# Attention's matmuls in pairs, a division on VectorE, unit lists from padded tables

## The reference, cut to what matters

```
h = relu(layernorm(x));  h = (h @ W.T).reshape(n, 8, 32)
enc   = relu(edge_attr @ edge_W.T + edge_b)            # 3 attributes per edge
alpha = sum(h[src]*a_src) + sum(h[dst]*(a_dst + enc))  # per edge and head
alpha = leaky_relu(alpha, 0.2)
ex    = exp(alpha - segment_max(alpha, dst)[dst])
out   = segment_sum(h[src] * ex / max(segment_sum(ex)[dst], 1e-10))
x = x + out + bias
h = relu(layernorm(x))
x = x + relu(concat(h, y1, y2) @ Wfc + bfc)            # y1, y2: two convolutions with batch norm
```

## Time and profile before

| | |
|---|---|
| median of 3 runs | 6951.39 us (6950.96 to 6955.41) |
| profiled execution, its span | 6959.5 us |
| PE, POOL, DVE, ACT busy | 69%, 71%, 51%, 30% of the span |
| unit lists | 0 to 119.5 |
| first dense stage | 119.5 to 308 |
| attention | 308 to 2614 |
| second dense stage | 2614 to 2808 |
| convolutions and end | 2808 to 6959.5 |

### The profile page before, as it was taken

The page is one execution under the profiler, slowest core; times in us unless marked ns, Lnnn a source line. Parts: engine busy times, 40 slices in busy tenths (PEclk is TensorE's granted clock), DMA queues, the critical chain, the costliest instruction groups (busy, mean ns, idle before and its releaser), DMA issues. The chain is left out here.

```text
span 6959.5 us, 113181 instructions
## 1 busy us (share of the span) xinstructions
PE 4805.8 (69%) x27409; PEld 3529.7 (51%) x27410; DVE 3523.0 (51%) x8745; ACT 2073.8 (30%) x5831; POOL 4908.5 (71%) x4806
## 2 busy tenths in 40 slices
PE   2699999999999994555555555556666666666655
PEld 1466666666666664344444444445544544444443
DVE  6688888888888888222222222223222222222224
ACT  3567777777777774000000000001000000000001
POOL 1777777776776756677777777774677777777775
PEclk9899999999999997555555555555555555555555
DMA  6777776777776655211111111111211111111115
GB/s 207 250 210 211 210 215 207 211 212 212 212 213 210 209 175 158 82 52 52 51 52 52 51 52 51 52 51 43 53 33 34 34 33 34 34 34 33 33 26 161
DMA packets 515795, 783.25 MB, mean 113 GB/s; under 512 B 143367, under 2 KB 392452, under 8 KB 514956
## 3 DMA queue, kind: packets, MB, share of 16 engines
q0 software_dynamic: 176176, 377.82, 21.0%
q1 hardware_dynamic: 303390, 369.82, 16.6%
q10 hardware_dynamic: 35758, 30.37, 1.4%
HBM read 695.07 MB, written 82.51 MB: 112 GB/s over the span
## 5 line engine op out<-in xcount | busy, mean ns | idle before, releaser
L1690 POOL DMA_INDIRECT c_g<-conv_table,c_idx x3128 | 3010.6, 962 | 1128.3 <-issue 952.9
L1767 PE MATMUL c_sums<-c_g,acc 128*128 x7040 | 1976.1, 441 | 1714.2 <-SPq L1653 1077.4
L1767 PEld LDWEIGHTS c_sums<-c_g,acc 128*128 128x128 f32 x7040 | 1626.4, 322 | 2220.1 <-issue 2210.1
L1002 POOL DMA_INDIRECT acc<-gat_table,ga_idx x1564 | 1615.8, 1033 | 653.0 <-issue 458.2
L1731 DVE TENSOR_TENSOR acc<-acc,c_sums 128x128 f32 (+1 forms) x1760 | 448.5, 255 | 2838.1 <-PE c_sums L1767 2821.7
L1386 PE MATMUL ga_sums<-ga_wg,ga_S 128*128 128x265 f32 x3520 | 999.3, 406 | 7.1 <-DVE ga_wg L1260 6.0
L1336 PE MATMUL ga_dstp<-ga_oht,ga_h 128*128 128x256 bf16 x5280 | 729.9, 275 | 76.0 <-DVE ga_prod L1181 69.7
L1386 PEld LDWEIGHTS ga_sums<-ga_wg,ga_S 128*128 128x128 f32 x3520 | 610.4, 193 | 171.4 <-issue 65.3
L1336 PEld LDWEIGHTS ga_dstp<-ga_oht,ga_h 128*128 128x128 bf16 x5280 | 505.7, 98 | 344.4 <-DVE ga_prod L1181 130.1
L1181 DVE SCALAR_TENSOR_TENSOR ga_prod<-acc,ga_a_dst,ga_dstp 128x512 f32<-128x512 f32 x880 | 645.0, 733 | 8.0 <-issue 6.7
L1077 ACT ACTIVATE ga_S<-iota_row,ga_dcol 128x128 f32<-128x128 f32 x1760 | 605.0, 392 | 73.5 <-issue 70.6
(11 more groups left out here) (253 smaller groups left out, 3731.5 us busy)
## 6 DMA issues: line engine op xcount, KB each, us to landing
ga_h<-h_parts SPq DMA_DIRECT2D x880, 192.0 KB
ga_dl<-dl_rows SPq DMA_DIRECT2D x110, 512.0 KB
c_g<-conv_table,c_idx POOLq DMA_INDIRECT x3128, 2.5
acc<-gat_table,ga_idx POOLq DMA_INDIRECT x1564
h_parts<-h_split SPq DMA_DIRECT2D x14, 1344.0 KB, 5.2
gat_table<-h_out SPq DMA_DIRECT2D x14, 952.0 KB
x_rows<-md_x SPq DMA_DIRECT2D x14, 896.0 KB, 7.1
fc_x<-x_rows ACTq DMA_DIRECT2D x98, 128.0 KB
```

The source lines that it names most:

```text
L1002: pool.indirect_dma_start(G[:, (v * PC + j) * HROW:(v * PC + j + 1) * HROW], None, gat_table, bass.IndirectOffsetOnAxis(idx[:, c:c + 1], 0 ...
L1690: pool.indirect_dma_start(G[:, c % (2 * SLOTS), :], None, table, bass.IndirectOffsetOnAxis(idx[:, c:c + 1], 0)).then_inc(rows_in[c // 2 % ...
L1767: last = nc.tensor.matmul(sums[:, b % R, 0:width], S[:, u * CH + 2 * b + j, :], flat[:, bass.ds(slots[b] * (2 * width) + j * width, width) ...
```

## The change

**Unit lists.** dst, `prev` and the attributes are no longer loaded and stored by way of SBUF. ACT issues copies from DRAM to DRAM into two padded tables, `pair_rows` (dst and prev of a pair, 2048 bytes) and `attr_pairs` (3072 bytes). SP loads only the last node of each pair (`tail_i`, 777 elements of 4 bytes) and src. POOL gathers seven times 128 rows of the one table, then of the other. The attributes are split behind the gathers, in whole tensors instead of halves.

**Dense routine.** rstd and shift have their own columns for each group, so `normal` no longer waits for earlier relus and copies nothing.

**Attention.** Only PE's `slot` is rewritten: steps of two. All other engines keep their order. Slot by slot PE has the same instructions.

**Second dense stage.** `share`, the multiplication by 1/denominator, goes from POOL to DVE, one group ahead. ACT copies `hT` for tiles 0 to 5 and DVE for tile 6.

**Counts.** `low_halves` reads the lower 16 bits of 32-bit numbers in three register loads.

```diff
+def low_halves(tab):
+    halves = tab.bitcast(U16)
+    return AP(halves.tensor, halves.offset, [list(halves.ap[0]), [2, tab.shape[-1]]])
...
-                for t, a, w in tables:
-                    sp.dma_start(t[0:PADDED, :], a[0:PADDED * UEPP * w].rearrange("(p e) -> p e", e=UEPP * w)).then_inc(s_loads, 16)
...
-                sp.wait_ge(s_rows, 3)
-                sp.dma_start(edge_rows.rearrange("(p q) e -> p q e", q=UQ), rows[:, :, :]).then_inc(s_rows_out, 16)
+                    sp.dma_start(tail_i[0:UFULL, :].rearrange("p (q o) -> p q o", o=1), AP(d.tensor, PAIR - 1, [[UEPP, UFULL], [PAIR, UQ], [1, 1]])).then_inc(s_tail_in, 16)
...
+                act.dma_start(pair_rows[0:FULL, 0, :], d[0:FULL * PAIR].rearrange("(p e) -> p e", e=PAIR)).then_inc(s_pairs, 16)
+                act.dma_start(pair_rows[1:FULL, 1, :], d[PAIR - 1:FULL * PAIR - 1].rearrange("(p e) -> p e", e=PAIR)).then_inc(s_pairs, 16)
...
+                act.dma_start(attr_pairs[0:FULL, :], a3[0:FULL * PAIR * 3].rearrange("(p e) -> p e", e=PAIR * 3)).then_inc(s_attr, 16)
...
-                pool.wait_ge(s_rows_out, 16)
                 pool.wait_ge(s_pair, 1)
+                pool.wait_ge(s_pairs, 16 * 9)
                 for q in range(UQ):
-                    pool.indirect_dma_start(rows[:, q, :], None, edge_rows,
+                    pool.indirect_dma_start(rows[:, q, :, :].rearrange("p n e -> p (n e)"), None, pair_rows.rearrange("u n e -> u (n e)"),
                                             bass.IndirectOffsetOnAxis(pair_i[:, q:q + 1], 0)).then_inc(s_gathered, 16)
+                pool.wait_ge(s_attr, 16 * 4)
+                for q in range(UQ):
+                    pool.indirect_dma_start(given[:, q, :], None, attr_pairs,
...
+                part(0)
+                store(0)
+                for n in range(TURNS, 2 * TURNS):
+                    take(n)
+                part(1)
+                store(1)
+                part(2)
+                store(2)
...
             def normal(g):
-                u = g % 2
                 dve.wait_ge(s_sd, g + 1)
-                if g >= 2:
-                    dve.wait_ge(relu_done, GT * (g - 1))
...
                 def slot(x, a, b, c, tail, more):

                     t, m, v = x.at(), x.at(-1), x.odd(-1)
-                    for k in range(QS):
-                        if k == 0 and tail:
-                            add(x.at(-3), UL - 1)
-                        if k and c:
-                            add(x.at(-2), k - 1)
+                    for k in range(0, QS, 2):
+                        for n in (k - 2, k - 1):
+                            if k == 0 and tail:
+                                add(x.at(-3), UL + n)
+                            if k and c:
+                                add(x.at(-2), n)
                         if b and k == 2:
                             lines(m)
                         if b and k == 4:
                             carries(m, v)
-                        if a and k < QS - 2:
-                            quantum(t, k + 2)
-                        if more and k >= QS - 2:
-                            quantum(t + 1, k + 2 - QS)
-                        if a and k % 2:
-                            dot(t, k - 1)
-                            dot(t, k)
                         if b and k == 6:
                             factors(m)
                             turn_back(m)
+                        for q in (k + 2, k + 3):
+                            if a and q < QS:
+                                quantum(t, q)
+                            if more and q >= QS:
+                                quantum(t + 1, q - QS)
+                        if a:
+                            dot(t, k)
+                            dot(t, k + 1)
                     if a:
                         close(x)
...
-                nc.gpsimd.tensor_tensor(heads, heads, spread(den, [[WROW, GT], [HCOLS, HEADS], [0, HDIM]]), ALU.mult).then_inc(scaled, 1)
                 pool.wait_ge(scaled, g + 1)
                 nc.gpsimd.tensor_tensor(heads, heads, spread(bias[:, :], [[0, GT], [HDIM, HEADS], [1, HDIM]]), ALU.add).then_inc(attended, 1)

+        def share(dve, g):
+            heads, den = columns(g)[:, :, :, 1:HCOLS], columns(g)[:, :, :, 0:1]
+            nc.vector.tensor_tensor(heads, heads, spread(den, [[WROW, GT], [HCOLS, HEADS], [0, HDIM]]), ALU.mult).then_inc(scaled, 1)
+
         def pre(dve, g, xg):
+            if g + 1 < GROUPS:
+                share(dve, g + 1)
             dve.wait_ge(attended, g + 1)
...
-by_act=(1, 3, 5)
+by_act=(0, 1, 2, 3, 4, 5)
```

More of the change, by code:

```diff
@@ L152, in gnn @@
         const = (iota_row, part_id, ident)
[L154 removed]
+        units_phase(nc, sb, ps, sem, held, A, const, pair_rows, attr_pairs, enc_parts, lists)
         end_phase()
@@ L271, in _ @@
-                sp.dma_start(prev_i[PADDED:UFULL, :], d[PADDED * UEPP - 1:UFULL * UEPP - 1].rearrange("(p e) -> p e", e=UEPP)).then_inc(s_loads, 16)
-                sp.dma_start(prev_i[UFULL:UFULL + 1, 0:UREST], d[UFULL * UEPP - 1:EDGES - 1].rearrange("(p e) -> p e", p=1)).then_inc(s_loads, 16)
+                d, s = A["dst"], A["src"]
+                sp.wait_ge(s_tail, 1)
+                with nc.allow_non_contiguous_dma(reason="the last node of each pair"):
+                    sp.dma_start(tail_i[0:UFULL, :].rearrange("p (q o) -> p q o", o=1), AP(d.tensor, PAIR - 1, [[UEPP, UFULL], [PAIR, UQ], [1, 1]])).then_inc(s_tail_in, 16)
+                    sp.dma_start(tail_i[UFULL:UFULL + 1, 0:UREST // PAIR].rearrange("p (q o) -> p q o", o=1),
+                                 AP(d.tensor, UFULL * UEPP + PAIR - 1, [[UEPP, 1], [PAIR, UREST // PAIR], [1, 1]])).then_inc(s_tail_in, 16)
@@ L333, in _ @@
                 nc.vector.tensor_copy(part_id[:, :], part_i[:, :])
[L334 to L337 removed]
+                link(nc.vector.tensor_copy(order[:, :], order_i[:, :]))
+                dve.wait_ge(s_tail_in, 32)
+                link(nc.vector.tensor_scalar(last_i[:, :], tail_i[:, :], 7, None, ALU.arith_shift_right))
                 link(nc.vector.tensor_scalar(last[:, :], last_i[:, :], float(TILES - 1), None, ALU.min))
                 nc.vector.tensor_tensor(last[:, :], last[:, :], order[:, :], ALU.add).then_inc(s_end, 1)
[L340 to L346 removed]
                 dve.wait_ge(s_end_in, 16)
@@ L413, in _ @@
             def _(act):
-                act.wait_ge(s_loads, 16 * LOADS)
-                for half in HALVES:
-                    nc.scalar.copy(left[:, half, :, :], attr[:, :].rearrange("p (q e f) -> p q f e", e=PAIR, f=3)[:, half, :, :]).then_inc(s_split, 1)
-                for n in range(PARTS):
-                    for k, half in enumerate(HALVES):
-                        if n:
-                            act.wait_ge(s_left, 2 * (n - 1) + k + 1)
-                        else:
-                            act.wait_ge(s_split, k + 1)
-                        nc.scalar.copy(part(n)[:, half, :, :], left[:, half, :, :]).then_inc(s_part if n < PARTS - 1 else s_rows, 1)
@@ L431, in _, with part, store @@
                     nc.scalar.copy(t[:, :].rearrange("e (p k) -> e k p", k=TURNS)[:, k, :], turn[:, n % 4, 0:P]).then_inc(s_taken, 1)
+                def part(n):
+                    if n:
+                        act.wait_ge(s_left, n)
+                        nc.scalar.copy(parts[:, n, :, :, :], left[:, :, :, :]).then_inc(s_part, 1)
+                    else:
+                        act.wait_ge(s_given, 16 * UQ)
+                        nc.scalar.copy(parts[:, 0, :, :, :], given[:, :, :].rearrange("p q (e f) -> p q f e", f=3)).then_inc(s_part, 1)
+                def store(n):
+                    act.wait_ge(s_part, n + 1)
+                    for f in range(3):
+                        act.dma_start(attr_rows[n * 3 + f, :].rearrange("(p q e) -> p q e", q=UQ, e=PAIR), parts[:, n, :, f, :]).then_inc(s_attr_out, 16)
+                for n in range(TURNS):
+                    take(n)
                 act.wait_ge(s_ew_rest, 1)
@@ L456, in dense_phase @@
     sd = sb(ctx, f"{name}_sd", [P, GT])
-    rstd = [sb(ctx, f"{name}_rstd{u}", [P, GT]) for u in range(2)]
-    shift = [sb(ctx, f"{name}_shift{u}", [P, GT]) for u in range(2)]
+    if keep is None:
+        keep = [sb(ctx, f"{name}_{n}", [P, TILES]) for n in ("rstd", "shift")]
+    rstd, shift = ([t[:, g * GT:(g + 1) * GT] for g in range(GROUPS)] for t in keep)
     if tp is None:
@@ L575, in relu @@
                     act.wait_ge(turn_done, GT * (g - NH) + a + 1)
-                nc.scalar.activation(hn[g % NH][:, a, :], xg[g % NX][:, a, :], ACT.Relu, bias=shift[g % 2][:, a:a + 1],
-                                     scale=rstd[g % 2][:, a:a + 1]).then_inc(relu_done, 1)
+                nc.scalar.activation(hn[g % NH][:, a, :], xg[g % NX][:, a, :], ACT.Relu, bias=shift[g][:, a:a + 1],
+                                     scale=rstd[g][:, a:a + 1]).then_inc(relu_done, 1)
             def copy(n):
@@ L1602, in load_frees @@
```

(2 more changed lines are left out.)

125 lines of the change are left out of this document (61 added, 64 removed).

## The result

The changed kernel takes 7064.14 us (median of 4 runs, 7061.88 to 7076.25) against 6951.18: a ratio of 1.0171, 95% interval 1.0156 to 1.0185. It is slower by 113 us. I had forecast slower, by 27, and 7064 lies above the range of 6875 to 7045. The profiled execution's span is 7074.5, 115.0 above that of before.

A forecast was written before the change was run, and what follows sets the result against it. In attention PE and DVE were taken to wait for each other, so order mattered. 88 − 36 − 25 = +27 us on the profiled 6959.5 gave 6986.5, less the span's 8.1 above the median: 6978, range 6875 to 7045.

The forecast's parts named there:

- 16-bit counts leave as many register loads as before: 0: Counts read into registers, part of the rest: no time gained or lost, 0 us, bounds −5 and +5.
- the loop: Attention: four alternating legs of PE and DVE, through adds, products, flushes and leaky, summing to 21.1 us a slot.
- Attention, +88: Attention: PE's paired order makes flushes wait for adds, +0.8 us in each of 110 slots; bounds −33 and +143.
- Second dense stage, −36: Second dense stage: multiplication moved to DVE, earlier first store, groups of 9.2 us; −36 us, bounds −45 and +5.
- Unit lists, −25: Unit lists: gathers start at 35, phase ends at 94 instead of 119.5; −25 us, bounds −32 and +5.
- 1 (the order costs nothing): Attention: PE is the bound and later flushes vanish in DVE's idle time; 6890 us, 6857 with full saving; chance 24%.
- 2 (POOL first): Second dense stage: POOL takes the shared ports first, about 3.1 us more a group; 7019 us in all; chance 8%.
- 3 (slow small loads): Unit lists: gathers start at 55 instead of 35, so the units gain only 5; 6998 us; chance 7%.
- 4 (7033): Attention: gathers wait longer for free blocks, 1.3 us lost a slot; 7033 us in all; chance 7%.
- my three terms: Attention +88, second dense stage −36 and unit lists −25, summing to +27 us.

The follow-up runs named there:

- single_32max: The changed kernel with PE's attention order of before and ACT's counts loaded as 32-bit numbers with a register maximum, against the kernel before: 6897.6 us, 0.9915.

## Why the prediction was wrong, point by point

- **"16-bit counts leave as many register loads as before: 0".** This is the step that failed, and it carries the miss. The term was 0, with bounds of −5 and +5; alone the load cost 49 us, and with the pairs 75 (7064 − 6989). The prediction counted loads and not their price, and gave as its reason that "no row shows an instruction waiting for them". There was one: in the view of waits of before, ACT's L1077 waits 69.9 us for "issue", 104 times, 0.67 us each, once in a slot and right where the registers are loaded. It was not among the rows I worked with, since ACT was not taken for a party in the loop. What the runs showed in place of the 0: eight 16-bit counts leave ACT idle for 1.83 us instead of 0.70, one-hot 3 comes later by that, and add 3 behind it.
- **Attention, +88.** Measured 91 with everything else equal. The loop of 21.1 is the 21.17 of the trace, and flush 2, flush 6 and leaky wait as said. That 88 comes so near is in part luck: +0.8 us a slot was chosen between +0.6 and +1.1, which are 66 and 121 us. And the reason given was half of it: I named only flushes 2 and 6 as what becomes late, and adds 0 and 4, now behind the wait for a product, are the larger part (53 against 36).
- **Second dense stage, −36.** Measured −46, at my bound of −45. My own working ended at 2764 for 2803.8, which is −40, and I took −36 from it. DVE had the ports first in each of the 13 groups where POOL's addition followed a multiplication, the intervals between stores were 8.6 to 8.9 us and not 9.2, until the last three, which are shorter, and the first store came 35.7 us after the phase's start (2816.24 − 2780.5) where I had 37. The usual group is no faster than the 8.46 of before. The gain lies at the start: the first store comes 25.5 us earlier in the stage, and the first three intervals are 8.7 us in the mean where they were 15.4 (SP's stores, 2675.21 to 2721.43 before).
- **Unit lists, −25.** Measured −11. The gathers start at 44.55, not at 35: the small loads land at 22.69, and a store and a load to the ends take another 8.5; 1.9 of these pass before SP issues the store at 25.15, right behind a load whose issuing ends at 25.10. The comparisons and sums take 13.4 us where I had 13. Then ACT's copy of the attributes (7.36) and DVE's first subtraction (7.45, with a step of three) follow one another from 68.16 to 83.01, where I had laid the copy beside DVE's list. Why the small loads take 22.69 us no run shows.
- **Rivals.** 1 (the order costs nothing) is refuted: the pairs cost 91 us. That a kernel without the load and the pairs takes 6898, near its 6890, says nothing for it. 2 (POOL first) did not happen. 3 (slow small loads) happened to about half: 14 us of the 25 are missing. 4 (7033) came nearest in time. Its sign is there, since POOL's gathers wait 366.0 us for weigh where they waited 110.9, but slower slots bring such a wait too, and what the runs show as the further loss is ACT's load.
- **Sum.** With 91 − 46 − 11 = +34 my three terms were 7 us off. With the 75 of the load they make 109 of the 113; the last 4 are within the intervals of the runs.

## What to carry to other kernels

Price every changed instruction, also those that the trace has no row for: a register load is an idle time ahead of the next instruction on its engine, and the type of the numbers counts as well as how many there are. Ask what stands behind it in the list, and put it where nobody waits. When the order of an engine is rewritten in pairs, look first for waits inside it: work that lay ahead of a wait and filled it is lost when it goes behind, even if the engine does the same work.

## What the runs showed of the hardware

Loading 16-bit numbers from SBUF into registers costs ACT about 0.21 us for each register (idle times of 0.39, 1.83 and 3.53 us with one, eight and sixteen), loading 32-bit ones an estimated 0.06 to 0.07 (0.70 us with eight in place of the 16-bit ones). The eight register maxima stand ahead of the copies of the source columns, L1085, and ACT has only 2.5 us of unnamed idle time there from 400 to 2580 (single_32max); so they cost nothing that these runs can tell. The change makes such loads 16-bit on POOL in attention and on PE and SP in the convolutions too. No loss shows there: with only ACT's loads and PE's order taken back the usual slot is 20.21 us (20.19 before the change), and the convolutions took 4147.5 us after and 4151.5 before.
